# Attention loop of a graph network on one core: a landing wait in front of every gather, with each landing counter split by parity

## The chip, the core and the metric

The program runs on one core of a Trainium2 chip. The core has five instruction streams that share only semaphores: TensorE (PE, with its weight loads shown apart as PEld), VectorE (DVE), ScalarE (ACT), GpSimd (POOL) and SyncE (SP). POOL issues all the indirect transfers (gathers and scatters), SP issues the plain ones. The metric is the device time of one launch in microseconds; lower is better.

## The reference

Four layers run one after another on 6250 nodes with 64 features and 206250 edges, sorted by destination. The change touches the third one, graph attention with 8 heads. Cut to what matters:

```python
h = (x @ W_att).reshape(n, H, D)
e = a_src[src] + a_dst[dst]
e = jnp.where(e > 0, e, SLOPE * e)
m = jax.ops.segment_max(e, dst, num_segments=n)
e = jnp.exp(e - m[dst])
s = jax.ops.segment_sum(e, dst, num_segments=n)
alpha = e / (s[dst] + SM_EPS)
msg = alpha[:, :, None] * h[src]
out = jax.ops.segment_sum(msg, dst, num_segments=n)
```

So for each edge the row of its source node is fetched, weighted with an exponential of the edge's logit, and summed over the edges of the same destination.

## The kernel before, in words

**Tiles and pieces.** The edges stand in T = 1612 tiles of 128, one edge per partition. The destination nodes stand in blocks of 16; a "piece" is the part of a tile that lies in one block. Since some tiles cross a block's end there are more pieces than tiles: 252 units of 8 pieces (QUAD = 8) against 202 tile units of 8 tiles (TU = 202). The loop over pieces is written out six units at a time (RING = 6) inside a hardware loop.

**The gathers.** For each tile one indirect transfer (`gather_tile`, L1600) fetches 128 rows of 77 numbers (64 features, a one, and the source logits as three bf16 parts) from `att_row_table` in HBM into the ring `tile_rows`, which holds 16 tile units (TRING = 16). It is issued by POOL and its landing raises one of four semaphores `s_tile` (TSEMS = 4) by 16; tile unit g uses number g mod 4. POOL's program is fully written out, with no loop. Before tile unit g it waits (L2158) until TensorE has read the ring slot's old tiles (semaphore `s_sum` against a number from the list `gates`, loaded every 8 units), and (L2161) until tile unit g - 4 has landed completely. Then its eight gathers follow with no wait among them. Twelve gathers (four that only prime the counters and tile unit 0) are issued ahead, in the block before the loop.

**SP** turns the landing counters into one counter: for each unit of pieces, six units ahead, `there` waits on all four `s_tile` (L2412) and raises `s_there` (L2413). Between these it issues the store of each finished unit, `piece_sums<-kept_l` (L2418).

**The chain of a unit of pieces.** ACT copies the logit parts of the tiles (L2182, after `s_there`); PE turns them (L2244) and spreads them over nodes and heads (L2255); DVE adds the destination's logit (L2318), ACT scales it (L2196), DVE takes the maxima (L2322 to L2341), ACT takes the exponentials (L2203, L2204); PE turns these (L2277), ACT copies them out of PSUM (L2210), PE multiplies them with the tile rows (L2269), and DVE adds the result to the running sums (L2367). The engines are skewed by one to three units, so a unit of pieces costs much less than the chain's length. What the order rests on is this written order on each engine and the semaphores; no scheduler is involved.

**Two other loops gather or scatter from POOL.** In the second layer's loop (L1295) the twelve gathers of a batch use two semaphores by parity, and from the third on each waits for the landing of the one two back. In the first layer's loop (L976) each scatter with addition waits for the one four back.

```python
for u in range(GP):
    if u > 1:
        e.wait_ge(s_grow[s][u % 2], i * 8 * GP + 16 * (u // 2))
        e.sem_inc(s_gpace, 1)
    e.indirect_dma_start(grow[s][:, u, :], None, h1_d, ...)
```

Of the kernel before, what the change touches and what calls it, by code (L numbers as in the profile page):

```python
# [23 lines left out]
NACC = 4  # L24
# [3 lines left out]
QUAD = 8  # L28
RING = 6
TRING = 16  # L30
TSEMS = 4
# [115 lines left out]
def build(nc, x, src, dst, edge_attr, edge_type, w0a, b0a, w0b, b0b, w1, b1, watt, att_s, att_d, batt, wf1, bf1, wf2,  # L147
          bf2, g1, be1, g2, be2, w3, b3, out):
    N, E = x.shape[0], src.shape[0]
    T = -(-E // (P * 2 * HALF)) * 2 * HALF  # L150
# [54 lines left out]
    with top:  # L205
# [3 lines left out]
        def sem(name, into=None):  # L209
            if into is None:  # L210
                return top.enter_context(nc.semaphore(name))
            into.append(nc.alloc_semaphore(name))
            return into[-1]

        def retire(sems):
            nc.clear_and_free_semaphores(sems)
            nc.all_engine_barrier()
# [92 lines left out]
        digits = sb("dst_digits", [P, 2 * T], f32, quads)  # L310
# [291 lines left out]
        with ExitStack() as ctx:  # L602
# [22 lines left out]
            def borrow(k, n, dt=f32):  # L625
# [15 lines left out]
            s_attr = [sem(f"l0_attr{h}") for h in range(2)]  # L641
            s_stage, s_psrc, s_eq, s_sum, s_val, s_hot, s_hist, s_dup, s_tgt, s_vfree, s_acc = (
                sem(f"l0_{n}") for n in ("staged", "src_rows", "equal", "summed", "values", "onehots", "hist",
                                         "dup", "targets", "val_free", "pace"))
            s_high, s_left, s_spread, s_z, s_dig, s_digits = (
                sem(f"l0_{n}") for n in ("high_parts", "rests", "spread", "z_added", "digits_staged", "digits"))
            s_add = [sem(f"l0_acc{k}") for k in range(NACC)]
            s_init, s_tail, s_pack = sem("l0_init"), sem("l0_tail"), sem("l0_packed")
            s_away, s_gap = sem("l0_digits_negated"), sem("l0_digit_distances")
            s_srow = [sem(f"l0_src_rows_loaded{h}") for h in range(2)]  # L650
            s_turn, s_turnc, s_turnst = (sem(f"l0_{n}") for n in ("src_turned", "src_turned_copied", "src_turned_stored"))
# [335 lines left out]
        with ExitStack() as ctx:  # L987
# [205 lines left out]
            retire(retired0)  # L1193
# [402 lines left out]
        s_tile = [sem(f"l2_tiles{k}") for k in range(TSEMS)]  # L1596
        EARLY = 1

        def gather_tile(e, t, to, k):
            e.indirect_dma_start(to, None, hx_d, bass.IndirectOffsetOnAxis(ap=src_col[:, t:t + 1], axis=0))\  # L1600
             .then_inc(s_tile[k], 16)

        with ExitStack() as ctx:
# [88 lines left out]
            with nc.Block() as block:  # L1692
# [37 lines left out]
                def _(e):  # L1730
# [27 lines left out]
                    for k in range(TSEMS):  # L1758
                        gather_tile(e, k, gathered[:, TRING - 1, k, :], k)
                    for g in range(EARLY):  # L1760
                        for r in range(QUAD):
                            gather_tile(e, g * QUAD + r, gathered[:, g, r, :], g)
# [337 lines left out]
        with ExitStack() as ctx:  # L2100
# [49 lines left out]
            with nc.Block() as block:  # L2150
                @block.gpsimd
                def _(e):
                    for g in range(EARLY, TU):
                        if g >= TRING:
                            if g % GATES == 0:
                                gates = loaded(gate[0:1, g:g + GATES], mybir.EngineType.Pool, 1, NQ)
                            e.wait_ge(s_sum, (gates[g % GATES] & 511) + SUMS0)
                            e.sem_inc(s_pace, 1)  # L2158
                        if g >= TSEMS:
                            e.wait_ge(s_tile[g % TSEMS], 16 * QUAD * (g // TSEMS) + 16)  # L2160
                            e.sem_inc(s_pace, 1)  # L2161
                        for r in range(QUAD):
                            gather_tile(e, min(g * QUAD + r, T - 1), gathered[:, g % TRING, r, :], g % TSEMS)
# [237 lines left out]
                def _(e):  # L2401
# [6 lines left out]
                    def there(groups):  # L2408
                        n = groups & 255
                        for k in range(TSEMS):  # L2410
                            e.wait_ge(s_tile[k], (((n + (TSEMS - 1 - k)) >> 2) << 7) + 16)
                            e.sem_inc(s_pace_sp, 1)  # L2412
                        e.sem_inc(s_there, 1)  # L2413
# [951 lines left out]
```

## Time and profile before

| | |
|---|---|
| time, median of 3 runs | 9646.02 us (9627.27 to 9649.23) |
| span of the profiled execution | 9754.5 us |
| busy share of the span: PE / PEld / DVE / ACT / POOL | 68% / 47% / 64% / 50% / 55% |
| gathers of the attention loop (L1600) | 1608 in the loop, started 3679.7 to 6579.9 us |
| copies of the weights `prob` (L2210), one per unit of pieces | 252, started up to 6727.4 us |

The profiled execution's time is known by its span alone, which is 1.1% over the median of the timed runs; sums below are made against the span and carried over to the median at the end. A row of the trace has a start, a duration, the engine and line, what is written and read, and in brackets how long the engine sat idle before it and what is taken to have released it. The name of a releaser can be wrong here: semaphores are freed after each layer and used again, so a wait in this loop can carry the name of a transfer of an earlier layer.

### The profile page before, as it was taken

How to read it: one execution, taken by the hardware profiler on the slowest of the kernel's cores; microseconds unless marked ns; L12 is line 12 of the kernel's file. 1: busy time of each engine (PE TensorE's matmuls, PEld its weight loads, DVE VectorE, ACT ScalarE, POOL GpSimd, SP SyncE). 2: the span in 40 equal slices, each digit the busy share in tenths (PEclk: the TensorE clock that was granted, in tenths of full speed). 3: DMA queues.
4: the chain of work that ended last, by engine and by line, in shares of the span. 5: the costliest groups of instructions: out<-in, count | busy, mean ns of one | idle time of the engine just before them, and what ended most of it. 6: DMA issues, size and time to landing. Idle time of an engine off the chain costs nothing. (4 is left out here: it accounts for less than half of the span.)

```text
span 9754.5 us, 145261 instructions
## 1 busy us (share of the span) xinstructions
PE 6607.5 (68%) x38830; PEld 4546.4 (47%) x38831; DVE 6236.8 (64%) x16834; ACT 4860.4 (50%) x11241; POOL 5337.6 (55%) x4893
## 2 busy tenths in 40 slices
PE   6988888875888852555555555557767666666665
PEld 3545545544777741445454444557533333333332
DVE  7999999986888832666676666668633333333333
ACT  5877777754777721333333333333334444444442
POOL 5888888873555545455555545551344444444444
PEclk9999999987888955555655555555577788888777
DMA  5444444441111112222222222222111111111111
GB/s 120 73 75 70 72 75 70 72 76 41 21 20 21 21 41 38 44 43 45 45 46 44 45 43 45 44 45 75 51 38 43 45 46 46 46 46 43 41 41 46
DMA packets 626461, 487.11 MB, mean 50 GB/s; under 512 B 513289, under 2 KB 530030, under 8 KB 616344
## 3 DMA queue, kind: packets, MB, share of 16 engines
q0 software_dynamic: 281600, 185.95, 15.9%
q1 hardware_dynamic: 342455, 293.43, 10.2%
q10 hardware_dynamic: 2304, 6.55, 0.3%
q8 instruction: 41, 0.67, 0.0%
q14 instruction: 61, 0.50, 0.0%
HBM read 303.43 MB, written 182.13 MB: 50 GB/s over the span
## 5 line engine op out<-in xcount | busy, mean ns | idle before, releaser
L1600 POOL DMA_INDIRECT tile_rows<-att_row_table,src_by_tile x1620 | 1528.4, 943 | 1413.6 <-PE banks L2269 763.7
L3027 POOL DMA_INDIRECT rows_l<-relation_table,idx x1302 | 1246.4, 957 | 1390.5 <-ACT idx L2967 1012.3
L976 POOL DMA_INDIRECT acc<-val,idx x1116 | 1722.6, 1544 | 378.9 <-issue 319.9
L3232 PE MATMUL banks<-h_parts,dense_onehot 128*128 128x448 bf16 x6510 | 1511.3, 383 | 553.0 <-issue 518.2
L2269 PE MATMUL banks<-tile_rows,prob 128*128 x4032 | 910.4, 402 | 1386.3 <-ACT prob L2210 595.5
L747 PE MATMUL banks<-part 128*128 128x490 bf16 (+1 forms) x7440 | 1569.6, 366 | 217.9 <-DVE part L830 209.8
L2269 PEld LDWEIGHTS banks<-tile_rows,prob 128*128 128x128 f32 x4032 | 831.8, 307 | 1480.6 <-issue 1480.3
L3232 PEld LDWEIGHTS banks<-h_parts,dense_onehot 128*128 128x128 bf16 x6510 | 643.0, 103 | 1334.6 <-issue 854.1
L747 PEld LDWEIGHTS banks<-part 128*128 128x128 bf16 x7440 | 694.3, 97 | 996.0 <-DVE part L830 270.4
L3144 DVE TENSOR_TENSOR h_nodes<-banks,dense_mask_j 128x448 f32<-128x448 f32 x310 | 192.9, 622 | 1476.3 <-remote 910.1
L2210 ACT COPY prob<-banks 128x1024 f32<-128x1024 f32 x252 | 255.0, 1012 | 1307.8 <-DMA quad_sums<-run 1076.4
L2318 DVE TENSOR_TENSOR banks<-banks,piece_att_dst 128x1024 f32<-128x1024 f32 x252 | 310.2, 1231 | 895.9 <-remote 877.9
L1295 POOL DMA_INDIRECT gathered_rows<-h_table,gathered_index x600 | 575.8, 960 | 545.3 <-issue 295.7
L906 ACT ACTIVATE digit_distance<-iota_row,dst_digits_negated 128x128 bf16<-128x128 f32 (+1 forms) x3224 | 868.7, 357 | 2.2 <-ACT dst_digits_negated L895 0.2
L1350 DVE TENSOR_SCALAR hot_src_lo<-columns_bf,codes 128x128 bf16<-128x128 bf16 x2300 | 613.6, 269 | 134.0 <-ACT codes L1414 59.4
L1453 ACT CAST counts<-banks 128x784 bf16<-128x784 f32 x650 | 522.2, 815 | 301.2 <-PE banks L1502 188.2
L830 DVE SCALAR_TENSOR_TENSOR part<-banks,src_digits,part 128x490 bf16<-128x490 f32 x992 | 671.2, 718 | 0.0
L1351 DVE TENSOR_SCALAR hot_code<-columns_bf,codes 128x196 bf16<-128x196 bf16 x2300 | 647.6, 285 | 0.0
L3003 ACT COPY run<-sums_by_feature 128x1664 f32<-128x1664 f32 x62 | 213.4, 3441 | 866.5 <-DVE sums_by_feature L3179 562.7
L2367 DVE SCALAR_TENSOR_TENSOR kept_l<-kept_l,fade,banks 128x65 f32<-128x65 f32 x2016 | 565.7, 281 | 117.9 <-issue 58.2
L1527 PE MATMUL banks<-counts,h_parts 128*128 128x208 bf16 x4900 | 630.0, 275 | 4.4 <-issue 4.2
L2196 ACT ACTIVATE edge_logit<-banks 128x1024 f32<-128x1024 f32 x252 | 257.8, 1023 | 569.8 <-DVE banks L2318 383.3
(449 smaller groups left out, 12370.0 us busy)
## 6 DMA issues: line engine op xcount, KB each, us to landing
src_rows<-src_by_column SPq DMA_DIRECT2D x63, 1152.0 KB
piece_sums<-kept_l SPq DMA_DIRECT2D x252, 264.0 KB
running_sums<-run SPq DMA_DIRECT2D x62, 832.0 KB
attr<-in_edge_attr SPq DMA_DIRECT2D x61, 624.0 KB
tile_rows<-att_row_table,src_by_tile POOLq DMA_INDIRECT x1620
rows_l<-relation_table,idx POOLq DMA_INDIRECT x1302
dense_code_rows<-src_by_column SPq DMA_DIRECT2D x62, 320.0 KB
acc<-val,idx POOLq DMA_INDIRECT x1116
```

What stands on the lines that cost most here:

```text
L747: last = e.matmul(ps[a][:, 0:ZW[a]], place0[(h * NZ + m) % 2][:, a, :], spread0[(h * NZ + m) % 2][n].rearrange("p b f -> p (b f)")[:, 0:ZW ...
L830: last = e.scalar_tensor_tensor(spread0[b][n], bc(ps[7][:, 0:ZB].unsqueeze(2), [P, ZB, W0]), dig[h][:, m, ZA:ZA + 1], bc(t.unsqueeze(1), [ ...
L906: last = e.activation(gap[n][:, r - a, :], iota[:, 0:w], ACT.Square, bias=away[n][:, r:r + 1])
L976: e.indirect_dma_start(acc_d[k], bass.IndirectOffsetOnAxis(ap=idx[h][:, r:r + 1], axis=0), val[h][:, r, :], None, compute_op=ALU.add).then ...
L1295: e.indirect_dma_start(grow[s][:, u, :], None, h1_d, bass.IndirectOffsetOnAxis(ap=gidx[s][:, u:u + 1], axis=0))\
L1350: e.tensor_scalar(hlo[slot(q)][:, u, :], cols[:, 0:P], code[s][:, 0, n:n + 1], None, ALU.is_equal)
L1351: last = e.tensor_scalar(hcd[slot(q)][:, u, :], cols[:, :], code[s][:, 1, n:n + 1], None, ALU.is_equal)
L1527: last = e.matmul(ps[4 + 1 - s][:, 0:BN * HT], parts4[:, m // 2, m % 2 * 2 * D:(m % 2 + 1) * 2 * D], table[1 - s][:, :, m // 2 * BN:(m // ...
L1600: e.indirect_dma_start(to, None, hx_d, bass.IndirectOffsetOnAxis(ap=src_col[:, t:t + 1], axis=0))\
L2269: last = e.matmul(summed(r), prob[u % 2][:, r, :], flat[:, bass.ds(cols[r], W1)], start=True, stop=True)
L3027: e.indirect_dma_start(g[h][:, r, :], None, y3_d, bass.IndirectOffsetOnAxis(ap=idx[h][:, r:r + 1], axis=0))\
L3232: last = e.matmul(ps[4 + b][:, 0:WJ], hot[h][:, k, m * P:(m + 1) * P], parts3[:, n, k * WJ:(k + 1) * WJ], start=(k == 0 and n == 0), stop= ...
```

## The change

Every gather of the loop from the third on now waits for the landing of the gather two before it. For that each of the four landing semaphores becomes a pair, by parity of the tile in its unit. The wait for the tile unit four back goes, since it follows from the new one. Priming the counters takes eight gathers instead of four. SP's `there` waits on eight semaphores instead of four. To have enough free semaphores, those of the first layer's loop are put in a list and freed after the first layer; this changes nothing else than the numbers that later semaphores get.

```diff
@@ -1190,7 +1191,7 @@
-            retire(retired0)
+            retire(l0_sems + retired0)
@@ -1593,12 +1594,12 @@
-        s_tile = [sem(f"l2_tiles{k}") for k in range(TSEMS)]
+        s_tile = [[sem(f"l2_tiles{k}_{n}") for n in range(2)] for k in range(TSEMS)]
         EARLY = 1
 
-        def gather_tile(e, t, to, k):
+        def gather_tile(e, t, to, k, n):
             e.indirect_dma_start(to, None, hx_d, bass.IndirectOffsetOnAxis(ap=src_col[:, t:t + 1], axis=0))\
-             .then_inc(s_tile[k], 16)
+             .then_inc(s_tile[k][n], 16)
@@ -1755,11 +1756,11 @@
-                    for k in range(TSEMS):
-                        gather_tile(e, k, gathered[:, TRING - 1, k, :], k)
+                    for k in range(2 * TSEMS):
+                        gather_tile(e, k, gathered[:, TRING - 1, k, :], k // 2, k % 2)
                     for g in range(EARLY):
                         for r in range(QUAD):
-                            gather_tile(e, g * QUAD + r, gathered[:, g, r, :], g)
+                            gather_tile(e, g * QUAD + r, gathered[:, g, r, :], g, r % 2)
@@ -2150,17 +2151,23 @@
+                    def landed(g):
+                        return 8 * QUAD * (g // TSEMS) + 16
+
                     for g in range(EARLY, TU):
                         if g >= TRING:
                             if g % GATES == 0:
                                 gates = loaded(gate[0:1, g:g + GATES], mybir.EngineType.Pool, 1, NQ)
                             e.wait_ge(s_sum, (gates[g % GATES] & 511) + SUMS0)
                             e.sem_inc(s_pace, 1)
-                        if g >= TSEMS:
-                            e.wait_ge(s_tile[g % TSEMS], 16 * QUAD * (g // TSEMS) + 16)
-                            e.sem_inc(s_pace, 1)
                         for r in range(QUAD):
-                            gather_tile(e, min(g * QUAD + r, T - 1), gathered[:, g % TRING, r, :], g % TSEMS)
+                            if r > 1:
+                                e.wait_ge(s_tile[g % TSEMS][r % 2], landed(g) + 16 * (r // 2))
+                                e.sem_inc(s_pace, 1)
+                            elif g > EARLY:
+                                e.wait_ge(s_tile[(g - 1) % TSEMS][r], landed(g - 1) + 8 * QUAD)
+                                e.sem_inc(s_pace, 1)
+                            gather_tile(e, min(g * QUAD + r, T - 1), gathered[:, g % TRING, r, :], g % TSEMS, r % 2)
@@ -2408,8 +2415,9 @@
                         for k in range(TSEMS):
-                            e.wait_ge(s_tile[k], (((n + (TSEMS - 1 - k)) >> 2) << 7) + 16)
-                            e.sem_inc(s_pace_sp, 1)
+                            for half in range(2):
+                                e.wait_ge(s_tile[k][half], (((n + (TSEMS - 1 - k)) >> 2) << 6) + 16)
+                                e.sem_inc(s_pace_sp, 1)
                         e.sem_inc(s_there, 1)
```

POOL's stream at the start of the loop, before the change. The names behind "waits" are those that a semaphore's number had first; quad_windows1 to 4 are the four `s_tile` here.

```order
L1600 DMA tile_rows<-att_row_table,src_by_tile 128x77 x24
L1600 DMA tile_rows<-att_row_table,src_by_tile 128x77 [waits quad_windows1]
L1600 DMA tile_rows<-att_row_table,src_by_tile 128x77 x7
L1600 DMA tile_rows<-att_row_table,src_by_tile 128x77 [waits quad_windows2]
L1600 DMA tile_rows<-att_row_table,src_by_tile 128x77 x7
```

The same place after the change; quad_windows3 and 4 are the pair of tile unit 1, l0_attr0 and l0_attr1 that of tile unit 2.

```order
L1601 DMA tile_rows<-att_row_table,src_by_tile 128x77 x2
L1601 DMA tile_rows<-att_row_table,src_by_tile 128x77 [waits quad_windows3]
L1601 DMA tile_rows<-att_row_table,src_by_tile 128x77 [waits quad_windows4]
L1601 DMA tile_rows<-att_row_table,src_by_tile 128x77 [waits quad_windows3]
L1601 DMA tile_rows<-att_row_table,src_by_tile 128x77 [waits quad_windows4]
L1601 DMA tile_rows<-att_row_table,src_by_tile 128x77 [waits quad_windows3]
L1601 DMA tile_rows<-att_row_table,src_by_tile 128x77 [waits quad_windows4]
L1601 DMA tile_rows<-att_row_table,src_by_tile 128x77 [waits quad_windows3]
L1601 DMA tile_rows<-att_row_table,src_by_tile 128x77 [waits quad_windows4]
L1601 DMA tile_rows<-att_row_table,src_by_tile 128x77 [waits l0_attr0]
```

No gather is moved past another; where one wait stood ahead of eight gathers, a wait now stands ahead of each. The second place is SP's loop, one unit of pieces, before the change:

```order
L2411 REGISTER_ALU
L2411 ISA
L2411 ISA [waits quad_windows1]
L2411 ISA [waits quad_windows2]
L2411 ISA [waits quad_windows3]
L2417 REGISTER_ALU [waits quad_windows4]
L2418 ISA [waits mlp0_h1_stored]
L2418 DMA piece_sums<-kept_l2_0 128x8x66
```

And after it:

```order
L2419 REGISTER_ALU
L2419 ISA
L2419 ISA [waits quad_windows1,quad_windows2]
L2419 ISA [waits quad_windows3,quad_windows4]
L2419 ISA [waits l0_attr0,l0_attr1]
L2425 REGISTER_ALU [waits l0_staged,l0_src_rows]
L2426 ISA [waits l0_src_rows_loaded0]
L2426 DMA piece_sums<-kept_l2_0 128x8x66
```

SP's order stays; each of its four waits becomes two.

## Rows read from the trace of the kernel before

**Rows 1.** Waits from 3640 to 6600 us: us in total, times, longest us.

```profile
ACT prob L2210 <- DMA quad_sums<-run: 1076.4, 135, 63.5
...
DVE banks L2318 <- remote: 877.9, 121, 47.6
...
POOL tile_rows L1600 <- PE banks L2269: 763.7, 95, 24.3
```

**Rows 2.** Timeline, 5003 to 5036 us, around one stall.

```profile
5010.62 0.94 POOL L1600 DMA_INDIRECT tile_rows<-att_row_table,src_by_tile  x1 [2.86 <-DMA gathered_rows<-h_table,gathered_index]
...
5014.56 1.91 PE L2277 MATMUL banks<-ident,run 128*128 128x128 f32 x8
...
5017.12 0.42 PE L2244 MATMUL banks<-ident_bf,tags_l 128*128 128x128 bf16 x2
...
5029.36 0.94 POOL L1600 DMA_INDIRECT tile_rows<-att_row_table,src_by_tile  x1 [0.30 <-issue]
5030.68 1.01 ACT L2210 COPY prob<-banks 128x1024 f32<-128x1024 f32 x1 [15.82 <-DMA quad_sums<-run]
```

**Rows 3.** Timeline of DVE, 3726 to 3773 us, near the loop's start.

```profile
3728.37 0.22 DVE L2344 TENSOR_TENSOR max_step<-max_step,running_max 128x8 f32<-128x8 f32 x1
3771.59 1.23 DVE L2318 TENSOR_TENSOR banks<-banks,piece_att_dst 128x1024 f32<-128x1024 f32 x1 [42.99 <-remote]
```

**Rows 4.** L2210's instructions from 6580 us on: count, first and last start.

```profile
L2210 ACT COPY prob<-banks x19: 1012/1012/1013, 6583.0 to 6727.4; 128x1024 f32<-128x1024 f32 x19
```

**Rows 5.** Longest waits of PE and DVE in the L1295 loop, 2400 to 3400 us.

```profile
PE banks L1502 <- ACT counts L1453: 82.8, 60, 3.9
...
DVE hot_src_lo L1350 <- remote: 48.3, 24, 5.0
```

**Rows 6.** Longest waits of PE in the L976 loop, 400 to 1900 us.

```profile
PE banks L747 <- DVE part L830: 157.8, 219, 1.1
```

**Rows 7.** The loop's gathers (3679 to 6581 us): count, min/median/max ns, idle before.

```profile
L1600 POOL DMA_INDIRECT tile_rows<-att_row_table,src_by_tile x1608: 938/944/964, 3679.7 to 6579.9; - x179
...
  POOLq L217: 25.9, 1
```

**Rows 8.** Timeline of POOL in the L1295 loop, 2798 to 2812 us.

```profile
2798.29 0.94 POOL L1295 DMA_INDIRECT gathered_rows<-h_table,gathered_index  x1 [1.04 <-DMA gathered_rows<-h_table,gathered_index]
2799.53 0.94 POOL L1295 DMA_INDIRECT gathered_rows<-h_table,gathered_index  x1 [0.30 <-issue]
2801.50 0.94 POOL L1295 DMA_INDIRECT gathered_rows<-h_table,gathered_index  x1 [1.02 <-DMA gathered_rows<-h_table,gathered_index]
2802.81 0.94 POOL L1295 DMA_INDIRECT gathered_rows<-h_table,gathered_index  x1 [0.37 <-issue]
```

**Rows 9.** The L1295 gathers from 2400 to 3400 us, with idle before.

```profile
L1295 POOL DMA_INDIRECT gathered_rows<-h_table,gathered_index x541: 938/943/1184, 2399.4 to 3393.3; - x181
...
  issue: 272.6, 454
...
  DMA gathered_rows<-h_table,gathered_index: 63.6, 65
```

**Rows 10.** The L976 scatters from 400 to 1900 us, with idle before.

```profile
L976 POOL DMA_INDIRECT acc<-val,idx x812: 1541/1542/1579, 399.7 to 1899.6; - x163
...
  issue: 231.5, 758
```

**Rows 11.** Windows: L1295 loop, L976 loop, attention loop with gathers, without.

```profile
core 0: us, PE busy (x) PEld busy (x) DVE busy (x) ACT busy (x) POOL busy (x), PEclk, DMA share, GB/s
2400.00:3400.00 1000.00, 873.58 (x8251) 768.97 (x8250) 827.99 (x4535) 732.46 (x1433) 513.51 (x541) 0.89 0.11 21
400.00:1900.00 1500.00, 1337.94 (x8236) 752.34 (x8233) 1406.23 (x3567) 1169.72 (x3557) 1251.25 (x812) 1.00 0.48 72
4000.00:6560.00 2560.00, 1365.15 (x7348) 1272.72 (x7349) 1702.37 (x4146) 939.84 (x2810) 1311.57 (x1391) 0.58 0.25 44
```

**Rows 12.** The page's DMA issues: count and KB each.

```profile
piece_sums<-kept_l SPq DMA_DIRECT2D x252, 264.0 KB
```

More of the change, by code:

```diff
@@ L640, in build @@
             src_z = src0f[:, 0:T].rearrange("p (h r) -> p h r", r=HALF)[:, :, HS:HALF]
-            s_attr = [sem(f"l0_attr{h}") for h in range(2)]
+            l0_sems = []
+            s_attr = [sem(f"l0_attr{h}", l0_sems) for h in range(2)]
             s_stage, s_psrc, s_eq, s_sum, s_val, s_hot, s_hist, s_dup, s_tgt, s_vfree, s_acc = (
-                sem(f"l0_{n}") for n in ("staged", "src_rows", "equal", "summed", "values", "onehots", "hist",
+                sem(f"l0_{n}", l0_sems) for n in ("staged", "src_rows", "equal", "summed", "values", "onehots", "hist",
                                          "dup", "targets", "val_free", "pace"))
             s_high, s_left, s_spread, s_z, s_dig, s_digits = (
[L646 to L651, printed above, removed]
+                sem(f"l0_{n}", l0_sems) for n in ("high_parts", "rests", "spread", "z_added", "digits_staged", "digits"))
+            s_add = [sem(f"l0_acc{k}", l0_sems) for k in range(NACC)]
+            s_init, s_tail, s_pack = (sem(f"l0_{n}", l0_sems) for n in ("init", "tail", "packed"))
+            s_away, s_gap = (sem(f"l0_{n}", l0_sems) for n in ("digits_negated", "digit_distances"))
+            s_srow = [sem(f"l0_src_rows_loaded{h}", l0_sems) for h in range(2)]
+            s_turn, s_turnc, s_turnst = (sem(f"l0_{n}", l0_sems) for n in ("src_turned", "src_turned_copied", "src_turned_stored"))
             assert TT * P >= T + HALF > (TT - 1) * P and 12 < TT < 17 and TT * P <= HS * P
```

## The prediction

> **What bounds the kernel now.** I read the page first, then the waits of each engine in the attention loop's stretch, then its timeline, then the same views of the two other loops in which POOL issues indirect transfers. The attention loop's gathers start from 3679.7 to 6579.9 us [rows 7], so the loop takes about 3050 us of 9754.5, and no engine is busy for more than two thirds of it: of the 2560 us from 4000 to 6560 DVE works 1702, PE 1365, POOL 1312 [rows 11]. Something makes them all wait. ACT waits 1076 us before copying `prob`, DVE 878 us before L2318, POOL 764 us for PE [rows 1].
>
> The timeline shows what such a wait is. From 5010.62 POOL issues one gather after the other, 0.94 us each with 0.30 us between, to 5029.36. PE's transposes L2277, which release ACT's copy L2210, are recorded at 5014.56 to 5016.47, but ACT goes on at 5030.68, after 15.82 us idle, just after POOL's last gather of that train ends at 5030.30 [rows 2]. All inputs were there; PE's work simply does not count as done while POOL's train of 16 gathers runs. Near the loop's start, where the ring is still empty and POOL may run without end, DVE once idles 42.99 us [rows 3].
>
> What the chain can do without gathers is seen after the last of them: 19 copies of `prob` start from 6583.0 to 6727.4 [rows 4], so 144.4 / 18 = 8.0 us for a unit of pieces. With gathers it is 2900 / 252 = about 11.5 us. So I read the loop as bound by stalls that POOL's trains cause, not by any engine's work and not by the gathers' bandwidth (the DMA share is 0.25 [rows 11]).
>
> Do stalls come with every gather beside busy engines? No. In the L1295 loop, where each gather from the third on waits for the one two back, POOL issues 541 gathers in 1000 us, about the attention loop's 1391 in 2560 (0.54 a microsecond in both) [rows 11], and the longest wait of PE is 3.9 us and of DVE 5.0 us [rows 5]. In the L976 loop POOL is busy 83% of the time (1251 of 1500 us), each scatter behind a wait, and PE never waits over 1.1 us [rows 6, 11]. The loops with a wait in front of each transfer have no stall of 15 us; the one with trains has them.
>
> **The change, part by part.**
>
> *Trains end.* If this reading is right, the stalls go, and the chain needs 8.0 us for a unit. That alone would be worth 252 x (11.5 - 8.0) = about 880 us. It is not had, because:
>
> *POOL becomes slower.* In the L1295 loop two gathers take 3.2 us (2798.29 to 2801.50, 2799.53 to 2802.81 [rows 8]), where trains take 2.5. On the whole of it, idle before a gather is 272.6 + 63.6 = 336.2 us over 519 gathers; taking out the one in twelve that has no wait (43 at 0.30 us) leaves 323.3 / 476 = 0.68 us, and with 0.95 us of work (513.5 / 541) that is 1.63 us for a gather that waits [rows 9, 11]. That is my lower bound. For the upper bound I take the slowest indirect transfer that POOL paces, the scatter at L976: 1.54 us of work and 231.5 / 758 = 0.31 us between, 1.85 us [rows 10]. The attention loop has more other traffic than L1295's (DMA share 0.25 against 0.11 [rows 11]: SP stores 264 KB for each unit of pieces [rows 12]), and a gather that lands late holds up both parities, since POOL goes through them in order. I choose 1.73 us, near the middle, 0.10 above what L1295 shows. That is a choice, not a reading.
>
> *The sum.* The loop has 1608 gathers, 1607 intervals, now 2900.2 us [rows 7]. At 1.73 us they take 2780 us, 120 less. POOL is then the bound: it delivers the 6.38 gathers of a unit of pieces in 11.0 us, and the chain needs 8.0, so the ring never fills and the gates (764 us of POOL's waits now [rows 1]) stop to matter. The stalls near the start cost nothing more either, since the chain only has to follow POOL.
>
> *The tail shrinks.* Now the chain is a ringful behind: 147.5 us pass from the last gather's start to the last `prob` copy (6579.9 to 6727.4 [rows 4, 7]). Afterwards it follows closely. The logit parts are copied two units ahead and `prob` two units behind, so about five units, 5 x 8.0 = 40 us, and some 5 us of landing remain: 45 us, 102 less.
>
> *The rest I cost at nothing.* Four more priming gathers, 4 x 1.25 = 5 us, lie in the block before, at whose end POOL idles 25.9 us for the others [rows 7]. If that cover were gone it would be 5 us. SP has eight waits where it had four for each unit; SP works six units ahead, and behind its waits only stands the store of a unit that was finished before. At 11 us a unit there is room for eight more short instructions. The list of first-layer semaphores only changes numbers. POOL's gate list is loaded every eight units, now behind a gather that is still being issued.
>
> Together: 120 + 102 = 222 us off the span, 9532. Carried over by the ratio of median to span (0.989) it is 220 us off 9646: 9426 us.
>
> With 1.63 us a gather it is 281 + 102 = 383, so 9267; with 1.85 it is -73 + 102 = 29, so 9617. Break-even is at 1.87 us.
>
> **Two rules of the Trainium skill.** The page SBUF — State Buffer, section on the two separate sides of SBUF, says that PE, ACT and DVE's own ports "never wait on anyone", and that a DMA cannot slow a compute op. By that rule the stalls have another cause than the trains and stay, and the change brings nothing; the trace of rows 2 speaks against it, and I keep it as a rival below. The page DMA: Bandwidth & Descriptors, section on the anatomy of a DMA from GpSimd, gives 2.0 us plus bytes / 436e3 for one; a gather of 39 KB would be 2.1 us by it, an estimate, which is less than two issues of 1.25 us, so POOL would not be slowed at all. The L1295 rows disagree with that outcome: 3.2 us for two.
>
> **Rivals.**
>
> *The stalls last a number of gathers, not a train (slower).* The stall of rows 2 spans 12 to 13 issues. If PE is held until so many descriptors are through, wait or no wait, each stall grows by 1.73 / 1.25 = 1.38. DVE's 878 us of waits then become 1215, 337 more: 9980. It decides if stalls of 12 us and more remain in the waits of ACT L2210. Against it stand both paced loops, which issue as densely and have none; for it, only that the cause of the hold isn't seen. 8%.
>
> *The stalls have nothing to do with the gathers (same).* They stay as they are, in place and length; POOL's 2780 us stay under the 2900 that the chain takes: 9646. For it speaks that the releaser named for ACT is no gather. Against: no stall after 6583 [rows 4], and the stall's end at the train's end. 5%.
>
> *POOL is not slowed (much faster).* With 1.25 us a gather the loop's gathers take 2009 us, as much as the chain: (2900 - 2009) + 102 = 993 less, about 8660. Against it rows 8 and 9. 3%.
>
> **How the numbers follow.** The forecast, stalls gone and POOL the bound at 1.63 to 1.85 us, has 84%, its own range being 9267 to 9617. For eight in ten I take 9290 to 9620: below lie the lowest cadences and the third rival, above the first two. About 0.3%, 29 us, is what a measurement of this kernel can tell from no change. Of the 84%, 3 fall within it (cadence near 1.85 or worse), 1 beyond it. So faster 0.80 + 0.03 = 0.83, same 0.03 + 0.05 = 0.08, slower 0.08 + 0.01 = 0.09.
>
> **What the profile after would show.** Right: no idle time over 6 us before ACT L2210 or DVE L2318 in the loop; idle time before the gathers of 0.6 to 0.9 us each, released by landings, and none by PE; gathers from about 3680 to about 6460; the last `prob` copy some 45 us after the last gather; the chain's units at about 11 us. Wrong in size: another mean interval than 1.73 us. Wrong in kind: long waits before L2210, or POOL waiting for PE at the gates, which would say that the chain is still the bound.

## The result, and the profile after

| | before | after |
|---|---|---|
| median of the timed runs, side by side on one chip | 9640.17 us | 9712.19 us |
| ratio to before, 95% interval | | 1.0071 (1.0057 to 1.0086) |
| the same in a later set of runs | 9766.67 us | 9812.79 us |
| ratio there | | 1.0047 (1.003 to 1.0065) |

The forecast was 9426 us, faster. The kernel became 0.5 to 0.7% slower.

Of what the prediction looked for, the kind is there and the sizes are not. No idle time over 6 us is left before `prob`, POOL waits for landings and nowhere for PE, and the last `prob` copy comes 44 us after the last gather. But the gathers end at 6667 us where 6460 was expected, a unit of pieces takes 3031.5 / 252 = 12.0 us where 11 was expected, and a gather waits 0.94 us in the mean where 0.6 to 0.9 was. The waits of the attention loop after the change (us in total, times, longest us):

```profile
ACT tags_l L2189 <- SPq L2421: 1281.5, 188, 9.9
...
POOL tile_rows L1601 <- DMA tile_rows<-att_row_table,src_by_tile: 1016.3, 637, 3.8
DVE banks L2325 <- PE banks L2262: 961.8, 155, 23.6
...
POOL tile_rows L1601 <- issue: 499.7, 969, 3.5
```

The 1076 us that ACT waited before `prob` and POOL's 764 us for PE [rows 1] are gone. ACT waits instead before the logit parts (L2189), the first step of a unit, for SP's word that the tiles have landed. The whole chain now waits for gathers: POOL is the bound. DVE waits for that first step too, before L2325 (L2318 before the change): 23.6 us once at the loop's start and up to 8.0 us later. That is over the 6 us that the prediction allowed there, but it is a wait for work that isn't done yet. The rest of ACT's waits before `prob`:

```profile
ACT prob L2217 <- PE banks L2284: 77.6, 59, 2.6
```

The loop's gathers after the change (count, min/median/max ns, first and last start), with what ended the idle time before them:

```profile
L1601 POOL DMA_INDIRECT tile_rows<-att_row_table,src_by_tile x1608: 938/942/994, 3635.8 to 6667.3; - x179
its engine sat idle before it (us, times) until:
  DMA tile_rows<-att_row_table,src_by_tile: 1016.3, 637
  issue: 500.0, 970
```

The `prob` copies behind the last gather:

```profile
L2217 ACT COPY prob<-banks x6: 1008/1012/1012, 6672.5 to 6711.3; 128x1024 f32<-128x1024 f32 x6
```

The tail is 6711.3 - 6667.3 = 44.0 us, where 45 were forecast. But 1607 intervals take 3031.5 us, 1.886 us each, where 1.73 were forecast and 1.85 was the upper bound; [rows 7] has 2900.2 us.

The span of the first profile of before, 9754.5 us, lay 114 us over the 9640.17 us that the same kernel takes beside the changed one. So both kernels were profiled once more on one chip (before_again and after_again, below; of before_again there is this one run). In that pair the gathers' row reads

```profile
L1600 POOL DMA_INDIRECT tile_rows<-att_row_table,src_by_tile x1608: 938/945/966, 3667.7 to 6557.0; - x179
```

before, with the last `prob` at 6705.3, and after the change

```profile
L1601 POOL DMA_INDIRECT tile_rows<-att_row_table,src_by_tile x1608: 938/942/992, 3677.4 to 6707.8; - x179
```

with the last `prob` at 6751.8. The loop takes 3030.4 instead of 2889.3 us, 141 more; the tail 44.0 instead of 148.3, 104 less. The sum is 37 us. The loop also starts 9.7 us later: the first gather of all comes 5.0 us later (3632.1 instead of 3627.1 us), and from it to the loop's first gather 45.3 us pass instead of 40.6, which is the time of the four more priming gathers. That makes 46.5 us up to the last `prob`, and the timed medians of that set differ by 46 us. Behind the last `prob` the changed kernel's profile is 20 us longer in this pair and 22 us shorter in the first one, so nothing there is counted.

**Why 1.886.** The timeline of POOL after the change, six gathers in a row (start us, duration us, in brackets idle time before and its releaser):

```profile
5002.80 0.94 POOL L1601 DMA_INDIRECT tile_rows<-att_row_table,src_by_tile  x1 [1.39 <-DMA tile_rows<-att_row_table,src_by_tile]
5004.05 0.94 POOL L1601 DMA_INDIRECT tile_rows<-att_row_table,src_by_tile  x1 [0.30 <-issue]
5005.98 0.94 POOL L1601 DMA_INDIRECT tile_rows<-att_row_table,src_by_tile  x1 [0.98 <-DMA tile_rows<-att_row_table,src_by_tile]
5007.30 0.94 POOL L1601 DMA_INDIRECT tile_rows<-att_row_table,src_by_tile  x1 [0.37 <-issue]
5011.43 0.94 POOL L1601 DMA_INDIRECT tile_rows<-att_row_table,src_by_tile  x1 [3.19 <-issue]
5012.68 0.94 POOL L1601 DMA_INDIRECT tile_rows<-att_row_table,src_by_tile  x1 [0.31 <-issue]
```

and SP's queue in the same stretch:

```profile
5008.88 0.38 SPq L2426 DMA_DIRECT2D piece_sums<-kept_l  x1
```

Most gathers follow in pairs, 1.25 us and then about 2 us apart. Once in each tile unit there is a hole, here of 4.1 us (5007.30 to 5011.43), and SP's store of the finished unit is issued inside it. (The trace writes "issue" beside this wait; by the code it is the wait of gather 3 for gather 1.) The store isn't there by chance. SP issues it behind `there`, which waits for the landing of a whole tile unit; so the last landing of one tile unit lets go ACT's work and the 264 KB store at once, just when the first gathers of the next tile unit are under way. In the trace the store is issued 1.2 us (median) after that landing. In 196 of 200 tile units one falls behind gather 0, 1 or 2; in the four others gather 1 lands after 2.14 us in the mean.

Averaged over the loop by a gather's place in its tile unit (landing: end of the last of its row transfers in the trace, less its start; interval: from the start of the gather ahead of it):

| place in the tile unit | 0 | 1 | 2 | 3 | 4 | 5 | 6 | 7 |
|---|---|---|---|---|---|---|---|---|
| landing, mean us | 2.15 | 3.25 | 2.92 | 2.30 | 2.17 | 2.15 | 2.16 | 2.16 |
| share that lands later than 2.6 us | 0% | 88% | 90% | 14% | 2% | 0% | 0% | 0% |
| interval, mean us | 1.36 | 2.10 | 1.35 | 3.56 | 1.36 | 2.08 | 1.33 | 1.94 |

A landing takes 2.17 us in the median, and a waiting gather starts 1.12 us (median) after the landing that it waits for: 3.29 us for two, 1.64 us each. Gather 1 is late in 88% of the tile units, and gather 3 waits for it. The late landing explains 3.25 + 1.12 - 1.35 = 3.02 of gather 3's 3.56 us. The rest lies behind the landing: gather 3 starts 1.68 us (mean) after gather 1's last row, not 1.12. That also goes with the store: it is 2.30 us with the store doubled and 1.13 us with the store in four parts (double_store and store4, below). What happens in that time the row transfers don't show. By the Trainium skill, page DMA: Bandwidth & Descriptors, anatomy of a DMA from GpSimd, one such transfer of 39 KB would take an estimated 2.1 us; the trace agrees, with 2.17 us from the start of the issue to the last row's landing. The 1.12 us behind it stand on top.

### The profile page after: what moved, and what is told of

Read it like the earlier page. It is cut to its first block and busy times, and to the rows that moved or that the text cites. A ratio compares the mean times of both kernels' runs of the same rounds, so it can differ in the third digit from the quotient of the medians.

```text
span 9716.0 us, 147687 instructions
## 1 busy us (share of the span) xinstructions
PE 6663.0 (69%) x38830; PEld 4555.6 (47%) x38831; DVE 6232.4 (64%) x16834; ACT 4872.9 (50%) x11241; POOL 5342.7 (55%) x4897
## 5 line engine op out<-in xcount | busy, mean ns | idle before, releaser
L2276 PE MATMUL banks<-tile_rows,prob 128*128 x4032 | 939.5, 408 | 264.3 <-DVE kept_l L2374 214.5
L2262 PE MATMUL banks<-tags_t_l,pick 128*128 128x128 bf16 x2016 | 259.4, 308 | 1138.1 <-ACT tags_t_l L2197 855.9
L2325 DVE TENSOR_TENSOR banks<-banks,piece_att_dst 128x1024 f32<-128x1024 f32 x252 | 310.4, 1232 | 983.2 <-PE banks L2262 968.8
L2189 ACT COPY tags_l<-tile_rows 128x24 bf16 x2016 | 250.3, 206 | 1336.4 <-SPq L2421 1290.3
L2262 PEld LDWEIGHTS banks<-tags_t_l,pick 128*128 128x128 bf16 x2016 | 204.4, 142 | 1213.0 <-issue 1164.2
```

Source lines behind the costliest of these rows:

```text
L2276: last = e.matmul(summed(r), prob[u % 2][:, r, :], flat[:, bass.ds(cols[r], W1)], start=True, stop=True)
```

## Experiments

All ratios are to the kernel before, timed beside it on the same chip. From one set of runs to another the kernel before took 9634 to 9882 us (9767 and 9634 us in two sets that name the same chip), so only ratios are compared between sets.

These theories come back in the expectations, all but the last on the stalls, which are also called holds. A: several gathers under way hold the other engines. B: the mere wait instructions break the stall. C: it is POOL's unbroken issuing, whatever is under way. D (later D'): it is how densely POOL issues; C' is that idle time is needed besides. S is a theory of the 1.886 us: the store, let go by the landing; its rival T, that the store's bytes cost the same wherever they fall.

**easy_waits: the same wait instructions, satisfied long before.** From the changed kernel:

```diff
-                            if r > 1:
-                                e.wait_ge(s_tile[g % TSEMS][r % 2], landed(g) + 16 * (r // 2))
...
+                            if g > 3:
+                                e.wait_ge(s_tile[(g - 4) % TSEMS][r % 2], landed(g - 4) + 8 * QUAD)
```

> The changed kernel with its eight counters, but the wait in front of each gather asks for a tile unit four back, which has long landed, so it never holds POOL. Theory A (what counts is that few gathers are under way or queued at once): the trains of 8 and 16 gathers at 1.25 us come back and with them the idle times of 15 us before ACT's copy of prob; the time is that of the kernel before, 9640 +- 60 us. Theory B (a wait instruction between the gathers is enough to let the other engines through): gathers at 1.25 us, no stall over 6 us, the chain at 8 to 9 us a unit, 9000 to 9150 us.

9891.99 us, ratio 1.0021 (0.9998 to 1.0044). The stalls are as before:

```profile
ACT prob L2214 <- DMA gathered_rows<-h_table,gathered_index: 1185.4, 142, 63.5
...
POOL tile_rows L1601 <- PE banks L2273: 765.2, 101, 23.9
```

The instruction changes nothing; POOL has to be slowed. B falls.

**back3 and back4: wait for the landing three or four back** (sixteen counters, by r % 4).

```diff
+                            gb, rb = divmod(g * QUAD + r - BACK, QUAD)
+                            e.wait_ge(s_tile[gb % TSEMS][rb % 4], 32 * (gb // TSEMS) + 32 + 16 * (rb // 4))
```

> The changed kernel with four counters for each tile unit, each gather waiting for the landing of the one three back. Theory A (trains hold the other engines because many gathers are under way): at most three are under way, so no stall over 6 us; three issues take 3.75 us, more than the 3.3 us from issue to the next one's start, so POOL runs at about 1.3 to 1.4 us a gather, the chain of 8.0 to 8.5 us a unit becomes the bound: 9000 to 9150 us. Theory C (it is POOL's unbroken activity that holds the others, however few are under way): the stalls are back, 9600 to 9700 us.

> As the last, but waiting for the landing four back. Theory A: like three back, 9000 to 9150 us, with stalls of a few us at most, as the loop with the scatters (four back) has. Theory C: stalls as before the change, 9600 to 9700 us.

back3: 9829.97 us, 0.9955 (0.9936 to 0.9974), ACT's longest wait before `prob` 58.8 us, 833 us in all. back4: 9895.97 us, 1.001 (0.9985 to 1.0036), 1233 us in all. At 1.25 us a gather, three issues (3.75 us) are longer than landing and waking (3.29 us), so such a wait is hardly ever real, and the trains stay. A's forecasts of 9000 to 9150 us missed by far for both. C's 9600 to 9700 us, as ratios to 9640 about 0.996 to 1.006, fit.

**double_store: a second store of every unit's sums**, to a table that nobody reads, beside the first, in the changed kernel.

```diff
+                        e.dma_start(twice_d[bass.ds(j * QUAD, QUAD), :, :].rearrange("k p f -> p k f"),
+                                    kept[u][:, :, :]).then_inc(s_twice[u], 16)
```

> The changed kernel with the store of each unit's sums issued twice, the second time to a table that nobody reads. If the 3.6 us interval that comes once in each tile unit is the store's packets holding up two gathers (0.26 us a gather over the 1.62 us of the bare round trip), a second store adds as much again or somewhat less: intervals of 2.05 to 2.15 us, 9712 + 260 to 420 = 9970 to 10130 us. If that interval has another cause, nothing or under 40 us is added.

10212.16 us, ratio 1.0341 (1.0299 to 1.0382). The time lies beyond the range expected, but that was worked out from 9712 us, and this chip is slower: before took 9882 us beside it instead of 9640. As ratios the range is 1.034 to 1.051, and the interval expected, 2.05 to 2.15 us, was met. The rows of the gathers:

```profile
L1602 POOL DMA_INDIRECT tile_rows<-att_row_table,src_by_tile x1608: 938/942/998, 3777.8 to 7094.3; - x179
its engine sat idle before it (us, times) until:
  DMA tile_rows<-att_row_table,src_by_tile: 1371.2, 747
```

2.064 us between gathers: the store's length does come through the landings into POOL's pace.

**before_again and after_again** are the two kernels on one chip. Their rows and times are shown above (before_again itself took 9764.06 us); both expectations were met.

> The kernel before, once more, for a profile on the same chip as the three others of this call. Both theories: as in the profile shown, trains of 8 and 16 gathers at 1.25 us, waits of ACT before the copy of prob of over 1000 us in all, last prob copy some 145 us after the last gather.

> The changed kernel, once more, on the same chip. Both theories: 0.2 to 1.2% slower than before, mean interval of the gathers 1.88 us, no idle time of ACT over 6 us before prob. If the ratio lies under 1 here, the result depends on the chip and the mis-sized term is the carry-over, not the cadence alone.

**pause4 and pause8: shorter trains.** Only gathers 0 and 4, or only gather 0, of each tile unit wait for the landing two back. (A wait before gather 1, left out here, asks for a landing two tile units back, which is long past.)

```diff
-                            if r > 1:
-                                e.wait_ge(s_tile[g % TSEMS][r % 2], landed(g) + 16 * (r // 2))
+                            if r == 4:
+                                e.wait_ge(s_tile[g % TSEMS][0], landed(g) + 32)
...
-                            elif g > EARLY:
-                                e.wait_ge(s_tile[(g - 1) % TSEMS][r], landed(g - 1) + 8 * QUAD)
+                            elif r == 0 and g > EARLY:
+                                e.wait_ge(s_tile[(g - 1) % TSEMS][0], landed(g - 1) + 8 * QUAD)
```

> As after, but only the gathers 0 and 4 of each tile unit wait for the landing of the one two back; the others follow at once. Trains of four. Theory C (a train of POOL's issues that isn't broken by idle time holds the others, the longer the train the longer the hold, and one idle microsecond ends it): cadence (3 x 1.25 + 2.0) / 4 = 1.45 us plus the store's share, about 1.5; no hold over 4 us; the loop's gathers take about 2420 us, tail some 45 us, so about 600 us less than before, ratio 0.93 to 0.95. Theory A (it is the number of gathers under way, two or fewer being harmless, that decides): never more than two are under way at a landing time of 2.2 us, so it says the same for landings alone; but with back3 it missed. Theory D (holds come from the share of time in which POOL issues, so that 1.88 us was needed): holds of 5 to 15 us stay, chain at 11 us for a unit, ratio 0.98 to 1.01.

> As pause4, but only gather 0 of each tile unit waits, so trains of eight with about one microsecond of idle time between. Theory C: holds up to about 6 us return, once for each train; chain at 9.5 to 11 us a unit, ratio 0.94 to 0.99, between pause4 and before. Theory D: as before, ratio 0.99 to 1.01, holds of 15 us and more. If pause8 has no holds over 4 us either and is faster than pause4, the length of a train below 16 does not matter.

pause4: 9521.22 us, 0.9756 (0.9721 to 0.9791). pause8: 9765.35 us, 1.0004 (0.9985 to 1.0024). Waits of pause4:

```profile
ACT prob L2220 <- DMA gathered_rows<-h_table,gathered_index: 740.1, 101, 17.5
```

and of pause8:

```profile
ACT prob L2217 <- DMA gathered_rows<-h_table,gathered_index: 975.8, 137, 64.7
```

An idle microsecond after four gathers doesn't end the stalls, as C had said it would; it shortens them. The ratio of pause4 lies between C's range (0.93 to 0.95) and D's (0.98 to 1.01), so both missed it; that of pause8 is the one that D expected and C did not.

**store4: the store in four parts.** The changed kernel; each part of two pieces is issued at another moment of the unit.

```diff
+                        for n, (s, ahead) in enumerate(((None, 0), (s_prob, 3), (s_slope, 5), (s_exp, 4))):
+                            if s is not None:
+                                e.wait_ge(s, done + {0: 1, 3: 2, 5: 1, 4: 3}[ahead])
+                            e.dma_start(piece_d[bass.ds(j * QUAD + 2 * n, 2), :, :].rearrange("k p f -> p k f"),
+                                        kept[u][:, 2 * n:2 * n + 2, :]).then_inc(s_kept[u], 16)
```

> As after, but the store of a unit's sums (264 KB in one transfer) goes in four transfers of two pieces each, the second to fourth behind waits for ACT's prob, slope and exponentials of the unit that the last landing set off, so that they come one after another over the unit. Theory S (the 0.25 us by which the gathers' mean interval, 1.886 us, is over the pair rhythm of 1.63 us come from the one long store, which the landing of each tile unit lets go onto the gathers 1 and 2 of the next): the late landings of gathers 1 and 2 (3.3 and 2.9 us against 2.15) go, mean interval 1.65 to 1.75, the loop's gathers 220 to 380 us shorter, ratio to before 0.965 to 0.985. Rival T (it is the bytes that cost, wherever they fall: each quarter delays the gather that it meets by its own time): mean interval 1.85 to 1.9, ratio 1.00 to 1.01.

9513.66 us, ratio 0.9823 (0.9806 to 0.9839). Its gathers:

```profile
L1601 POOL DMA_INDIRECT tile_rows<-att_row_table,src_by_tile x1608: 938/942/971, 3678.0 to 6475.9; - x179
```

2797.9 / 1607 = 1.741 us, with the same bytes and the same waits; gathers 1 and 2 land after 2.46 and 2.28 us in the mean instead of 3.25 and 2.92. T is out; S holds, for 0.145 us of the excess.

**pause3 and pause3_store4, pause4_store4:** waits before gathers 0, 3 and 6, with the store whole and in parts, and trains of four with parts. Gathers 0 and 1 have the waits of pause4.

```diff
-                            if r > 1:
+                            if r == 3 or r == 6:
                                 e.wait_ge(s_tile[g % TSEMS][r % 2], landed(g) + 16 * (r // 2))
```

> Waits before the gathers 0, 3 and 6 of each tile unit, the store in one transfer as in the kernels before and after. pause3_store4 was at 0.967. Theory S (the one long store makes the gathers under it late, and each waiting one then costs about a microsecond): mean interval 1.70 to 1.75 instead of 1.64, ratio 0.98 to 0.985. If the store's form makes no difference to trains of three: 0.965 to 0.97.

> Waits before the gathers 0, 3 and 6 of each tile unit (trains of three, three and two), store in four parts. Theory C (holds grow with the train's length): holds shorter than with trains of four, POOL at (5 x 1.25 + 3 x 2.05) / 8 = 1.55 us for a gather, so that the loop takes 1607 x 1.55 to 1.62 = 2490 to 2600 us and the tail 45 to 100: ratio 0.95 to 0.965, the fastest. If holds don't depend on length between three and four, 0.97 to 0.98 like pause4.

> Trains of four gathers and the store in four parts. Since pause4 was bound by the chain with its holds (its tail was 141 us), and less by POOL, the store's parts help little by theory S: ratio 0.965 to 0.98 (pause4 alone was 0.976). If holds come from the long store as well, clearly under 0.96.

pause3: 9593.17 us, 0.9797 (0.9748 to 0.9846). In another set of runs pause3_store4: 9363.22 us, 0.9672 (0.9655 to 0.9688), and pause4_store4: 9505.94 us, 0.9815 (0.9796 to 0.9835). With trains of three (pause3) ACT's longest wait before `prob` is 5.1 us, and the parts bring the mean interval from 1.743 to 1.638 us. With trains of four, where the chain is the bound, the parts bring nothing; pause4 alone was 0.9756, on another chip. Both ratios with parts lie just above their ranges (0.965 and 0.98).

**The fillers: POOL never idle, gathers further apart.** The kernel before, with all its trains, plus a memset by POOL after each gather of the loop, into a tile that nobody reads; WIDTH is 256, 320, 384 or 448. (The wait keeps one memset behind the other.)

```diff
                             gather_tile(e, min(g * QUAD + r, T - 1), gathered[:, g % TRING, r, :], g % TSEMS)
+                            if g * QUAD + r > EARLY * QUAD:
+                                e.wait_ge(s_unread, g * QUAD + r - EARLY * QUAD)
+                            e.memset(unread[:, :], 0.0).then_inc(s_unread, 1)
...
+            unread = sb("unread", [P, WIDTH], f32, ctx)
```

> The kernel before, plus one memset of 128 x 256 by POOL into a tile that nobody reads after each gather of the loop, so that POOL is never idle but issues a gather only every 1.6 us or so. Theory C (only idle time of POOL, or landings waited for, ends a hold): waits of ACT before prob stay, over 800 us in all, with single ones of 15 us and more. Rival D (it is the density of issues that holds the others; 1.6 us apart they do no harm): waits before prob fall below 300 us in all and none is over 6 us, gathers at 1.6 us, faster than before by 2 to 4%.

> The kernel before plus one memset by POOL after each gather, of 128 x 448 where the run with filler had 128 x 256 (0.33 us, gathers 1.44 us apart). About 0.57 us each, so gathers 1.67 us apart with POOL never idle. Theory D' (what holds the others is how densely gathers are issued; the hold shrinks steadily with the distance): waits of ACT before prob fall from filler's 831 us to below 300, none over 6 us, POOL never waits for PE, POOL the bound: loop 1607 x 1.67 = 2684 us, tail 45 us, ratio to before 0.96 to 0.975. Theory C' (idle time is needed as well): waits before prob stay at 800 us, chain still the bound, ratio 0.97 to 0.98 with a tail of 140 us.

> The kernel before plus a memset of 128 x 384 after each gather: 0.44 us, so gathers about 1.55 us apart (1.44 us with 128 x 256 had the chain as the bound, 1.60 us with 128 x 448 had POOL). If the bound is still POOL: last gather at 3665 + 1607 x 1.55 = 6155 us, tail 45 us, ratio to before 0.945 to 0.95. If the holds are back: waits of ACT before prob over 400 us, tail over 100 us, ratio 0.955 to 0.97.

> The same with 128 x 320: 0.38 us, gathers about 1.49 us apart. If the hold shrinks steadily with the distance, this lies between: chain and POOL about equal, tail 45 to 140 us, ratio 0.94 to 0.965. If there is a sharp edge between 1.44 and 1.60 us, either 0.935 to 0.945 with no waits before prob, or 0.965 to 0.975 as filler.

> The kernel of the run filler with the store in four parts. With filler the chain is the bound, and no gather waits for a landing, so by theory S the store's parts change little: ratio 0.965 to 0.98. If the store's burst takes part in the holds, below 0.96.

> The wide memset and the store in four parts. By theory D' POOL is the bound at 1.67 us with or without the parts: as filler_wide within 0.5%.

| width | us between gathers in a train | ACT's longest wait before `prob` | SP's register and semaphore instructions over 0.5 us, 4000 to 6580 us | ratio to before |
|---|---|---|---|---|
| none (before_again) | 1.25 | 63.4 | 558 of 2715 | 1 |
| 256 (filler) | 1.44 | 12.7 | 400 of 2792 | 0.973 (one run) |
| 320 | 1.49 | 6.7 | 275 of 2658 | 0.9445 (0.9419 to 0.947) |
| 384 | 1.55 | 3.1 | 6 of 2659 | 0.9503 (0.948 to 0.9526) |
| 448 (filler_wide) | 1.60 | 3.1 | 8 of 2713 | 0.9538 (0.9498 to 0.9578) |

The two 3.1 us are from behind the last gather; before it ACT waits 1.8 us at most. With 256, 830.8 us of waits remain:

```profile
ACT prob L2215 <- DMA gathered_rows<-h_table,gathered_index: 830.8, 149, 12.7
```

Neither C nor D had filler right: C wanted single waits of 15 us and more, D none over 6 us, gathers 1.6 us apart (they came at 1.44). The wider memsets were tried for that. With the widest POOL's timeline is this:

```profile
5000.85 0.95 POOL L1600 DMA_INDIRECT tile_rows<-att_row_table,src_by_tile  x1 [0.16 <-issue]
5001.79 0.50 POOL L2168 MEMSET unread<- 128x448 f32 x1
5002.45 0.94 POOL L1600 DMA_INDIRECT tile_rows<-att_row_table,src_by_tile  x1 [0.17 <-issue]
```

its gathers and ACT's longest waits:

```profile
L1600 POOL DMA_INDIRECT tile_rows<-att_row_table,src_by_tile x1608: 942/950/987, 3668.9 to 6242.3; - x179
...
ACT tags_l L2187 <- SPq L2418: 748.9, 121, 9.1
```

filler_320's gathers:

```profile
L1600 POOL DMA_INDIRECT tile_rows<-att_row_table,src_by_tile x1608: 941/950/1002, 3639.8 to 6047.5; - x179
```

and its waits before `prob`:

```profile
ACT prob L2215 <- DMA gathered_rows<-h_table,gathered_index: 450.8, 114, 6.7
```

With the widest memset there is no wait for a landing, no idle time of POOL over 1.0 us, and no stall. C falls. D holds: the stalls go by how far the issues stand apart. With filler_wide, gathers 1 and 2 land as late as in the changed kernel (3.45 and 3.01 us, late in 97% and 87% of the tile units), and it costs nothing, since no gather waits for them: the intervals are 1.59 to 1.64 us at every place.

filler_store4 (9591.12 us, 0.9813, 0.9774 to 0.9852) and filler_wide_store4 (9361.49 us, 0.9557, 0.9519 to 0.9594) show the other side: where no gather waits, the store's parts bring nothing, and with the chain as the bound they seem to cost. They also do more than spread the store: SP issues them behind waits for ACT, and only then goes on to say that the next tiles have landed. From filler to filler_store4 the row of ACT's waits before `prob` falls from 831 to 243 us, and 757 us of waits before L2187, the first step, come up instead; pause4_store4 has the same. So in these two runs what the parts bring and what they cost can't be told apart.

Between 1.44 and 1.55 us ACT's longest wait shrinks steadily. filler_320 is where both bounds meet: the chain is still held a little, its tail is 6116.8 - 6047.5 = 69 us, and it is the fastest kernel of all, **9108.68 us beside 9634.11, 5.5% less.** The changed kernel's own idea, waiting for landings, gave at best 0.967.

## Why the prediction was wrong, point by point

*Stalls come from POOL's trains, and end with them:* right. No engine waits 15 us for finished work any more [rows 2], and in both profiles POOL waits for PE nowhere in the loop. What ends them was read too narrowly: the wait isn't needed, only the distance between issues. Trains at 1.60 us stall nobody. The prediction missed that since it compared means, 0.54 gathers a microsecond in both loops [rows 11], and took them for equally dense; in the attention loop this mean holds the idle time at the gates, and within a train the gathers are 1.25 us apart.

*POOL becomes the bound:* right; the chain waits for landings in its first step.

*The tail shrinks by 102 us:* right, 104 in the pair on one chip.

*"I choose 1.73 us, near the middle":* **this is the step that failed.** 1.886 us was measured. The term is +141 us where -120 stood, and it alone turns the sign. The prediction named the store as other traffic and said that a late landing holds up both parities, and then spread it as an average between two loops that have no such store (in the first SP stores 64 KB at a time, 45 times in 1000 us; in the second it only loads). It did not ask when the store is issued. The order of the code answers that: it stands right behind `there`, so each landing of a tile unit lets it go. What it does to gathers stood in the trace of before: there all 127 gathers of the loop that start within 1 us after the issue of a store land later than 2.6 us (3.17 us in the mean), and of the 705 that start over 4 us away from any store, 1%. In before nobody waits for them; the change puts a wait behind every one. Three runs show this term: store4, which cuts the store in four and moves the parts apart in time, comes to 1.741 us; filler_wide, with the same late landings and no waits on them, to 1.60; double_store to 2.064. What was left out is the product of the two: a burst tied to a landing, and a wait tied to the gathers that it makes late.

*The upper bound of 1.85* came from a loop whose transfers are longer (1.54 us) and whose waits lie four back; it bounded nothing here. The nearest row, 1.63 us for two under way [rows 9], plus one long store for each tile unit would have been the better sum.

*The priming gathers* were costed at nothing, with POOL's 25.9 us of idle time at the block's end as cover. That cover isn't one: POOL idles 25.6 us there after the change as well, and the four gathers cost 4.7 us.

*The carry-over from span to median* was harmless in kind: break-even at 1.87 us in the profile shown, (2889.3 + 104.3) / 1607 = 1.863 in the pair on one chip. Against both, 1.886 is slower.

*The rivals.* That stalls last a number of gathers: no, they went. That they have nothing to do with gathers: no. That POOL isn't slowed: no. The slower outcome came by the forecast's own mechanism with a larger number, to which 1 in 100 was given; the margin from 1.85 to 1.87 deserved much more.

Not settled: the remaining 0.10 us between store4's 1.741 and the pair rhythm of 1.64. Quarters still meet gathers (gathers 1 and 4 land after 2.46 and 2.47 us), which argues for the same cause; no run took the store away. The list of first-layer semaphores wasn't tried alone; up to the last `prob` the pair on one chip leaves it at most the 5.0 us by which the first gather comes later, and these may be chance.

## What to carry to other kernels

A wait for a landing makes an issuing engine pay for every late landing, so before adding one, ask which transfers are let go by that same landing: such a burst hits the next gathers every time, not on average. If the aim is only to slow the issuing engine down, space its issues with a small instruction that waits for nobody, and choose its width where the stalls and the engine's own pace meet. Profile before and after on one chip when a few parts in a thousand decide.

## What the runs showed of the hardware

POOL's indirect transfers hold the other engines by how densely they are issued: ACT's longest wait before `prob` is 63.4 us at 1.25 us between issues and 12.7 at 1.44; at 1.55 us no such stall is left. pause4, where four gathers and a pause take about 5.8 us, 1.45 us for each, behaves much like the filler at 1.44 (740 and 831 us of waits, longest 17.5 and 12.7 us). This suggests that a mean over some gathers matters and not single distances. How many gathers are under way changes together with the distance (2.17 us to land is 1.7 of them at 1.25 us and 1.4 at 1.60), and no run parts the two. By the Trainium skill, page SBUF — State Buffer, two separate sides, PE, ACT and DVE's dedicated pair of ports "never wait on anyone". These rows show engines waiting, though nothing here shows that SBUF is the place of it.

Even SP, which only waits and issues here, is slowed: of its register and semaphore instructions one in five takes over 0.5 us (median 0.71) with trains at 1.25 us, and 8 of 2713 at 1.60 us. So what is held may be the instruction streams or their semaphores, not the arithmetic; that is a guess. What POOL's issuing takes from them, no run here shows.

A gather that waits for a landing starts 1.12 us after it, in the median. Behind the store it is 1.68 us in the mean (gather 3 of a tile unit in the changed kernel), and 2.30 us behind two stores.
